# ScalarE loads the other function's table early: one column of GELU behind the last exponential, one of Exp behind the last GELU

## What is computed

```python
# block 1
xm1 = _ln(x) * (1 + scale_sa) + shift_sa
q, k, v = split(xm1 @ qkv_w + qkv_b)
x = x + gate_sa * (softmax(q @ k.T * SCALE) @ v @ sa_proj_w + sa_proj_b)
qc = _ln(x) @ q_w + q_b;  kc, vc = split(context @ kv_w + kv_b)
x = x + softmax(masked(qc @ kc.T * SCALE)) @ vc @ ca_proj_w + ca_proj_b
xm3 = _ln(x) * (1 + scale_ff) + shift_ff
x = x + gate_ff * (gelu(xm3 @ fc1_w + fc1_b) @ fc2_w + fc2_b)
# block 2: the same three parts, with q and k rotated, no mask, no gates
```

## Time and profile before

| | |
|---|---|
| median of three runs | 1698.59 us |
| the profiled execution's own time | 1698.97 us |
| its span, first to last instruction | 1697.1 us |
| PE busy | 1521.9 us, 90% of the span |
| PE weight loads busy | 1326.5 us, 78% |
| DVE busy | 1093.2 us, 64% |
| ACT busy | 940.3 us, 55% |
| POOL busy | 722.4 us, 43% |
| mean granted TensorE clock | 0.960 of full |

### The profile page before, as it was taken

The page is one execution under the profiler, slowest core; times in us unless marked ns, Lnnn a source line. Parts: engine busy times, 40 slices in busy tenths (PEclk is TensorE's granted clock), DMA queues, the critical chain, the costliest instruction groups (busy, mean ns, idle before and its releaser), DMA issues.

```text
span 1697.1 us, 44731 instructions
## 1 busy us (share of the span) xinstructions
PE 1521.9 (90%) x17760; PEld 1326.5 (78%) x17760; DVE 1093.2 (64%) x2373; ACT 940.3 (55%) x1689; POOL 722.4 (43%) x982
## 2 busy tenths in 40 slices
PE   4979899898999989899898998989899898989987
PEld 3868878787887878788787787878878787887866
DVE  4556666566666656667667676666666667676654
ACT  3456565655655556555655645556454565655533
POOL 3133424233242432425547455454554546455411
PEclk9899999999999999999998999999999999999978
DMA  6110100101010010101110100000000000000000
GB/s 209 46 45 10 45 15 15 52 13 54 7 40 22 16 51 13 42 15 44 40 45 26 42 11 26 11 29 8 20 14 14 26 11 17 18 23 2 2 14 13
DMA packets 34251, 49.39 MB, mean 29 GB/s; under 512 B 3488, under 2 KB 24928, under 8 KB 34048
## 3 DMA queue, kind: packets, MB, share of 16 engines
q1 hardware_dynamic: 34048, 46.54, 8.9%
HBM read 38.07 MB, written 8.45 MB: 27 GB/s over the span
## 4 chain that ended last, share of the span: by engine, by line
PE 70%; DVE 14%; issue 7%; ACT 7%; POOL 1%; DMA 0%; SPq 0%; DVEq 0%; POOLq 0%; ACTq 0%
PE score_t L665 8%; PE score L647 8%; PE p_unit L541 6%; PE p_mix L707 5%; PE p_unit L543 5%; PE p_unit L542 5%; PE p_unit L734 5%; DVE neg_max L1098 3%; PE p_out L541 3%; PE p_out L543 3%; PE p_out L542 3%; PE p_out L696 2%; PE p_mix L572 2%; PE score_t L542 2%; PE score_t L541 2%
## 5 line engine op out<-in xcount | busy, mean ns | idle before, releaser
L1098 DVE TENSOR_REDUCE neg_max<-score 128x8 f32<-128x1024 f32 x224 | 273.7, 1222 | 167.4 <-PE score L647 159.0
L647 PE MATMUL score<-k_t,q_t 32*128 32x256 f32 x1792 | 268.7, 419 | 63.6 <-DVE q_less L1108 28.6
L665 PE MATMUL score_t<-q_less,k_t 32*128 32x128 f32 x3584 | 278.9, 297 | 11.6 <-ACT probs_t L965 6.2
L665 PEld LDWEIGHTS score_t<-q_less,k_t 32*128 32x128 f32 x3584 | 234.6, 199 | 23.4 <-issue 14.9
L647 PEld LDWEIGHTS score<-k_t,q_t 32*128 32x128 f32 x1792 | 171.3, 197 | 102.7 <-issue 47.7
L967 ACT ACTIVATE probs_t<-score_t 128x1024 f32<-128x1024 f32 x168 | 172.2, 1025 | 102.5 <-PE score_t L665 89.7
L887 ACT ACTIVATE xt<-p_mix,mod_now 128x128 f32<-128x128 f32 x384 | 154.7, 455 | 104.3 <-PE p_mix L572 74.7
L1301 POOL TENSOR_TENSOR xt_lo<-xt,xt_hi 128x256 fp32r<-128x256 f32 x128 | 96.5, 754 | 256.5 <-ACT xt_hi L892 256.4
L734 PE MATMUL p_unit<-w_out,heads_t 128*128 128x256 f32 x512 | 145.0, 406 | 15.9 <-ACT q_t L931 8.2
L1144 DVE CAST hid_hi<-hid 128x256 fp32r<-128x256 f32 x256 | 96.3, 376 | 91.0 <-ACT hid L952 90.7
L541 PE MATMUL p_out<-w_hi,hid_lo 128*128 128x256 f32 x512 | 147.6, 288 | 0.8 <-issue 0.8
(11 more groups left out here) (157 smaller groups left out, 4249.7 us busy)
## 6 DMA issues: line engine op xcount, KB each, us to landing
ctxt<-in_ctxT SPq DMA_DIRECT2D x16, 512.0 KB, 3.8
side<-gates SPq DMA_DIRECT2D x15, 512.0 KB, 5.7
x_new<-in_x SPq DMA_DIRECT2D x32, 128.0 KB, 2.1
x_mid<-xs SPq DMA_DIRECT2D x8, 512.0 KB, 3.6
x_new<-x_mid SPq DMA_DIRECT2D x32, 128.0 KB, 2.0
out<-xs SPq DMA_DIRECT2D x8, 512.0 KB, 2.9
k_t<-in_L_f_wT SPq DMA_DIRECT2D x2, 1024.0 KB, 5.7
probs_t<-in_L_xcond_fc_w SPq DMA_DIRECT2D x1, 1024.0 KB, 10.3
```

The source lines that it names most:

```text
L647: mm = pe.matmul(score_banks(b, h)[:, r % 2, t * 2 * N:(t + 1) * 2 * N].rearrange("p (e n) -> p e n", e=2), q_t[s][rows(r), t, tokens], k_ ...
L665: mm = pe.matmul(turned_banks(b, h)[:, r % 2, x * N:(x + 1) * N], k_t[s][rows(r), t, e, tokens], q_less[rows(r), j % 2, t, e, :], start=Tr ...
L1098: dve.tensor_reduce(by_half[:, 2 * h:2 * h + 2, :, :, 0], score_banks(b, h)[:].rearrange("p r (t e n) -> p r t e n", t=CT, e=2), AX.X, ALU ...
```

## The change

Two activations of one column of `cond`, 128 partitions x 1, are added on ACT, behind the exponentials and GELUs of a step and ahead of its `move_heads`. One is a Gelu, in step 35 of each group, which is step 9 of the next one, right behind that one's last self attention exponential. The other is an Exp, in step 42, right behind the group's last GELU. Their output `primed` is read by nothing, and they wait for nothing. The program has one table load more than before, 33 where it had 32, since each group now has both, the last one too. Nothing is moved on any other engine.

```diff
+PRIME_GELU = PERIOD + AT_EXP + 2 * GB - 2
+PRIME_EXP = [max(steps) for steps in GELU_AT]
 LAST = MLP_FROM + max(len(_counts) for _counts in MLP_COUNTS) + 1
...
+        primed = sb("primed", [P, 1])
...
                         for n in GELU_AT[layer_of(group)].get(step, ()):
                             gelu(group, n)
                     for group, step in live(t):
+                        if step == PRIME_GELU:
+                            act.activation(primed[:], cond[:, 0, 0:1], ACT.Gelu)
+                        elif step == PRIME_EXP[layer_of(group)]:
+                            act.activation(primed[:], cond[:, 0, 0:1], ACT.Exp)
+                    for group, step in live(t):
                         for s, b in batch_at(step, AT_TURN_BACK + ACT_HI):
                             move_heads(group, 4 * s + b)
```

## The result

The change takes the kernel from 1698.28 us (median of four runs, 1695.87 to 1701.22) to 1670.28 us (four runs, 1669.28 to 1671.03). The ratio is 0.984, 95% interval 0.9822 to 0.9857: 28 us faster, where 17.8 us were forecast. The direction was right. Run again on another chip, the change took 1670.32 us, with a ratio of 0.9856 (0.9828 to 0.9885).

The account below looks back on a forecast made before the run. PE's work was taken as the base, with time won or lost where PE waits. Terms -9.0 - 11 - 2.5 - 3.2 + 7.7 + 0.2 = -17.8 us from 1698.97 gave 1681 us, range 1673 to 1694.

Parts of the forecast that it names:

- Layer 1, Gelu to Exp, -9.0 us: Seven places before layer 1's first masked exponential: moving the load away saves PE 1.29 us each, -9.0 us.
- The clock in layer 1, -11 us: Same seven places: a shorter PE wait can leave TensorE's clock up, -11 us, bounds 0 and -15.3.
- the clock stays down: Layer 1's clock falls although PE waits only 1.4 us; sum -6.8, time 1692 us, chance 0.18.
- Exp to Gelu, layer 1, -2.5 us: Seven layer 1 places: GELU starts 1.3 us earlier, PE's wait for `z` gives back 0.35 us each, -2.5 us.
- Exp to Gelu, layer 2, -3.2 us: Eight places in layer 2 and at the boundary: DVE's first split starts 0.4 us earlier each, -3.2 us.
- Layer 2's clock, taken as it is: Layer 2: PE's clock falls behind the wait ending at 1120.54, for DVE's `q_less`; left unchanged, with no term.
- Layer 2, Gelu to Exp, +7.7 us: Seven layer 2 places: the formerly hidden load now delays `modulate` and PE, 1.1 us each, +7.7 us.
- The new row: Sign in layer 2: PE waits at L572 for ACT's `xt`, about 0.95 us each in 6 or 7 places.
- clock lost at the new stops: Layer 2's new PE stops cost clock: 1690 us with layer 1's clock recovered, chance 0.12; 1704 without, chance 0.07.
- A switch of 2.66 us: Rival by the Trainium skill: each function switch takes 2.66 us including a drain; sum -14.6, 1684 us, chance 0.02.
- the +0.2: The end of the kernel: the last group's Gelu load stays, with a column of 0.2 us behind it, +0.2 us.
- its two named reasons: Grounds for the range's low end, 1673: layer 1's clock gain near its 15.3 us bound, and layer 2's smallest loss.

## Why the prediction was right or wrong

- **Layer 1, Gelu to Exp, -9.0 us: right, a little small.** PE's wait went from 1.64 to 0.19 us, 1.45 us a place and 10.2 us in all, since the exponential also overlaps `q_t`. The cover for the load in its new place held at L577, by the trace.
- **The clock in layer 1, -11 us: right in kind, perhaps somewhat small.** The Exp columns of layer 1 alone gave 21.0 us by the medians and 23.3 us between the row maxima, so the clock is the 11 to 13 us beside 10 us of wait. In the change the falls are gone from all seven stages. But the ground for it was weak, and that all seven stages kept the clock was in part luck. I compared with a 1.82 us wait without a fall and took 1.4 us for safe. In truth 1.2 us (1.0 + 0.2) was free of falls and 1.5 us had five of seven. The rival "the clock stays down", with 0.18, was 0.3 us of wait away.
- **Exp to Gelu, layer 1, -2.5 us: too large.** The columns gave 0.1 us a place, 0.7 us in all, and PE still waits about 0.28 us for `z`. The heads were just in time, as forecast. What failed is that DVE's chain would keep its length when it starts earlier: its splits then run beside POOL and take 0.8 us.
- **Exp to Gelu, layer 2, -3.2 us: mis-sized, 4.7 us.** The split starts some 0.6 us earlier a place, not 0.4, since ACT's keys, heads and mix overlap each other by 0.1 us when they run back to back. PE waits 1.17 us for `z` where it waited 1.82 us.
- **Layer 2's clock, taken as it is: the step that failed.** "PE's clock falls behind the 1120.54 wait before, and I leave that as it is" looked at one place only, and the sum has no term for layer 2's clock. The profile before has falls at PE's wait for `z` too, at 985 and 1292, that a shorter wait could take away. In layer 2 the clock stood at its lower level for 87.5 us before and 77.6 us after. Those 10 us at half clock are up to 5 us of PE's time. The kernels with and without Gelu columns show the cause: 87.5 and 88.1 us without, 77.2, 77.5 and 77.5 us with them, where no Exp column disturbs layer 2. Where one does, the same quantity goes from 66.9 to 77.6 us in two traces of the change, so how much of it came in one run of the change is partly chance, and stays open.
- **Layer 2, Gelu to Exp, +7.7 us: right in kind, somewhat large.** 6.0 us by itself, 1.0 us in each of six places, not 1.1 in seven. The new row stands where it was forecast, with 0.85 us for 0.95. The rivals built on it (clock lost at the new stops, 0.12 and 0.07) didn't occur.
- **A switch of 2.66 us: wrong here.** The Trainium skill (ScalarE: Activation LUTs, What ACT_TABLE_LOAD costs) puts a drain behind each load and 2.66 us on a switch in all. Here the 33 loads take 1.28 us each, and behind those of the switches the next instruction starts after 0.01 us. The rival's sum of -14.6 also left out the -3.2 and the +0.2; with them it is -17.6, so it could not have been told from the forecast by the time.

In all, the prediction had +4.7 us for layer 2 and the end, and it was -2.7 us. That is 7.4 of the 10.1 us by which the profiled execution missed: some 5 us of clock, 1.5 us of layer 2's Gelu columns and 1 to 2 us of its Exp columns. The other 2.7 are 0.7 us by which the start of the two executions differs, 1.2 us more from the waits, 1.8 us less from layer 1's Gelu columns, and for the rest the clock of layer 1. The low end of the range, 1673, lay only 2.5 us beyond what its two named reasons give (1675.5), and neither was a gain of clock in layer 2.

## What to carry to other kernels

A table load costs nothing where its engine idles and its full length where the function behind it is already due, so place it by what follows it in the trace, one place at a time: the same move gave 3.0 us a place in layer 1 and cost 1.0 us a place in layer 2. An engine that starts earlier can come to lie beside another and slow down, so follow its chain to the wait that it ends. When PE waits near a fall of its clock, price every wait of the pattern for the clock too, also those that the change shortens by the way, and take the comparison from waits that stand together as these do, not from a single longer one. A dose of small delays shows in two or three runs how near the edge a kernel stands.

## What the runs showed of the hardware

- TensorE's clock fell behind two waits of 1.0 and 0.5 us that stood close together in five stages of seven, and behind 1.0 and 0.2 us in none. A single wait of 1.82 us left it up at 19 of 28 places (5, 7, 4 and 3 of seven in four traces), and one of 0.9 to 1.2 us at all 70. The same stage, with waits alike, falls in one period and not in the next.
- A fall in the stages of layer 1 lasts 3.4 us or twice that (a granted clock of 0.79 or 0.57 over 8 us, at 1.2 GHz instead of 2.4: 0.21 x 8 x 2 and 0.43 x 8 x 2), and costs 1.4 to 1.5 us for each 3.4 us.
- One column of an activation takes 0.20 us, and about 0.1 us of it overlaps its neighbours. A table load takes 1.28 us, and the next instruction, where its data are there, starts 0.01 us behind it.
- DVE's splits of a GELU's output (128 x 256) take 0.3 to 0.4 us, and 0.8 us beside POOL's instructions: in layer 1, 25 of 192 without the Gelu columns and 37 with them, all of the slow ones while POOL was busy. Another 24 lay beside POOL and were not slowed.
